# A new slot table for the state-space stage, three banks for its scans, and y in two banks by turns

## The chip, the cores and the metric

The program runs on one core of one Trainium2 chip. The metric is the device time of one execution in microseconds; lower is better.

## What is computed

Four layers follow one another on x (8 x 512 tokens of 256), each as x = x + layer(layernorm(x)): linear attention, a mixture of eight experts with one expert per token, a state-space layer, and the mixture of experts again. Only the state-space layer is touched. Cut to what matters:

```
xc, z = split(x @ in_proj_w.T)
u  = conv over 4 taps (512 -> 512 channels) of xc, + conv_b
dt = clip(sigmoid(u @ dt_w.T + dt_b), 1e-4, 1)
B, C = u @ B_w.T, u @ C_w.T                    # 16 states each
for every t:
    state = exp(dt * A) * state + dt * B * u + 1e-6     # 512 channels x 16 states
    y = sum over states(state * C) + D * u
out = (y * silu(z)) @ out_w.T
```

All of it is float32.

## The kernel before

Channels lie on partitions and time along the free axis, so the recurrence over 512 time steps of one quarter k (128 channels) and one state n is a single scan instruction on VectorE (DVE), `m_scan`, L1047. There are 8 batches x 16 states x 4 quarters = 512 scans. The program is written in **slots**: slot g = 64 b + 4 n + k holds scan g, and 64 slots are a batch b. The engines run their own instruction streams side by side and meet at semaphores.

What every slot holds:
- ScalarE (ACT): `m_decay`, exp(dt * A) for the scan three slots ahead (L612, ring of five buffers), and `m_input`, one of the four pieces of dt * B * u for the next group of four scans (L622).
- TensorE (PE): `m_spread`, four 128x128 transposes (L1091) that turn the input of scan g into a PSUM bank, 2 or 3 by turns, where the scan reads it. It waits for the scan two slots back.
- DVE: the scan. Its result goes into one of seven h buffers (the list H).
- GpSimd (POOL), once every four slots: `c_product` (L407) multiplies the four h quarters of state n by C; states 2 to 13 are then added onto state 0 or 1 by an accumulating DMA of 1 MB (`add_on`, L419), the last two by a sum on POOL (L417). A DMA waits for the last but one before it. SyncE (SP) loads the row of C for each state (L340), and in between stores the finished rows of the batch before.

Everything else of the layer is fitted between the scans, at slots that tables of numbers set; every engine walks through the same table in order:
- `CONV_AT`, `BC_AT`, `DT_AT`, `Z_AT`, `OUT_AT`: the slots at which PE issues the matmuls of conv (L1327), of B and C (L1341), of dt (L1359) for batch b + 1, of z (L1391) for b, and of the output of b - 1 (L1411, 256 wide, two of which count as one here). `UT_AT`, `DTT_AT`, `BT_AT`, `XT_AT`: turns by transposes of u (L1335), dt (L1376), B (L1369) and x.
- `UC_AT`, `UTC_AT`, `BCC_AT`, `TH_AT`, `ZTH_AT`, `NORM_AT`, `XTC_AT`: ACT's evacuations, the two passes of dt (L596, L598), the tanh of z (L604) and the norm.
- `SKIP_AT`, `ADD_AT`, `FINAL_AT`, `UPDATE_AT`, `CLIP_AT`, `WT_AT`, `BTC_AT`, `GATE_AT`: DVE's passes. y of a batch is made in PSUM in four banks, 4 to 7, one for each quarter: `m_skip` writes D * u (L988), `m_add` adds the even and the odd sum of POOL (L999), `m_final` multiplies by the gate (L1005). `m_clip` (L965) and `m_weigh` (L977) belong to dt, `m_gate` (L983) to z, `m_update` (L1014) adds the output matmul to x and then takes its statistics (L1020).

All matmuls other than the spreads share banks 0 and 1, so many wait for a bank that ACT or DVE has yet to read:

```
CONV_AT = ((0, 0, 1, 2, 2, 3, 4, 4), (5, 6, 6, 7, 8, 8, 9, 10), (10, 11, 12, 12, 13, 14, 14, 15),
           (16, 16, 18, 18, 20, 20, 22, 22))
DT_AT = ((32, 32, 34, 34), (40, 40, 41, 42), (46, 46, 47, 48), (52, 52, 53, 54))
DTT_AT = (38, 45, 51, 57)
TH_AT = (35, 43, 49, 55)
CLIP_AT = (36, 44, 50, 56)
```

Before the first scan the same table is walked for batch 0 alone (`m_prep(0, q)`), and behind the last one come the adds, finals and outputs of batch 7.

## Time and profile before

| | |
|---|---|
| median of 3 runs | 1716.4 us (1714.13 to 1721.19) |
| the profiled execution, its own time | 1717.43 us |
| its span, first to last instruction | 1715.3 us |
| mean granted TensorE clock | 0.925 |
| busy: PE, DVE, ACT, POOL | 85%, 65%, 56%, 53% of the span |
| DMA | 202.87 MB, mean 118 GB/s |

The profile is of one execution. Busy shares are over the whole program, in which the state-space layer is about one half; the profile's slices and the stretches that are asked of the trace tell the layers apart. In a row of the trace, what stands behind "idle before" is the time for which the engine stood still before the instruction, and the arrow names what ended it.

### The profile page before, as it was taken

Reading aid. Unit: us, or ns where it says so; the run is one execution under the profiler, and the core shown is the slowest. Engines: PE = TensorE matmul, PEld = TensorE weight load, DVE = VectorE, ACT = ScalarE, POOL = GpSimd, SP = SyncE. Lnnn points to the kernel's source line nnn. Section 1 sums busy time; section 2 is a strip of 40 time slices with the busy share of each in tenths; the row PEclk is TensorE's granted clock in tenths of the full one; section 3 lists DMA queues with packets and bytes.
Section 4 is the critical chain, followed back from the end, with each engine's and each line's share of the span. In section 5 each row is a group of like instructions: output and inputs, shape, how many; then the busy total and the mean of one; then the engine's idle time right before and its main releaser. Section 6 shows DMA issues by size and latency. Waiting matters only on the chain.

```text
span 1715.3 us, 21255 instructions
## 1 busy us (share of the span) xinstructions
PE 1453.1 (85%) x6310; PEld 930.3 (54%) x6311; DVE 1120.5 (65%) x1703; ACT 957.8 (56%) x1749; POOL 913.6 (53%) x417
## 2 busy tenths in 40 slices
PE   2899787999996978989889899898997773859997
PEld 1566584666642545545545555455554552836664
DVE  5566536444341677988878889888898985354443
ACT  1222120333323888888888888988888880203332
POOL 1111001344200578979879788797887995014442
PEclk9999958999998989999999999999999587579999
DMA  9300022111130386694966949759488495601120
GB/s 304 125 24 24 25 74 71 49 60 59 30 98 13 71 191 132 153 207 99 217 144 151 199 101 214 171 133 202 102 198 189 108 227 136 211 25 56 60 59 19
DMA packets 81315, 202.87 MB, mean 118 GB/s; under 512 B 9610, under 2 KB 40463, under 8 KB 68689
## 3 DMA queue, kind: packets, MB, share of 16 engines
q0 software_dynamic: 21376, 119.30, 32.3%
q1 hardware_dynamic: 55632, 78.91, 14.8%
q10 hardware_dynamic: 4224, 3.67, 0.7%
q8 instruction: 38, 0.62, 0.1%
q14 instruction: 45, 0.36, 0.1%
HBM read 84.14 MB, written 18.88 MB: 60 GB/s over the span
## 4 chain that ended last, share of the span: by engine, by line
PE 61%; DVE 15%; ACT 10%; issue 8%; DMA 2%; POOL 2%; SPq 1%; ACTq 1%; DVEq 0%; POOLq 0%
PE ps L1091 11%; PE ps L1261 8%; PE ps L1244 8%; PE ps L1327 7%; DVE arena L1047 6%; PE ps L1359 5%; ACT arena L612 4%; ACT arena L622 4%; PE ps L1116 3%; PE ps L1391 3%; PE ps L1296 3%; PE ps L1153 2%; PE ps L1107 2%; PE ps L1341 2%; PE ps L1189 2%
## 5 line engine op out<-in xcount | busy, mean ns | idle before, releaser
L1091 PEld LDWEIGHTS ps<-cst,arena 128*128 128x128 f32 x2836 | 361.2, 150 | 353.6 <-issue 216.0
L1091 PE MATMUL ps<-cst,arena 128*128 128x128 f32 x2836 | 461.0, 292 | 106.4 <-DVE arena L1047 31.3
L407 POOL TENSOR_TENSOR arena<-arena 128x2048 f32<-128x2048 f32 x98 | 450.1, 4594 | 162.0 <-DVE arena L1047 161.0
L1047 DVE TENSOR_TENSOR_SCAN arena<-arena,ps 128x512 f32<-128x512 f32 x392 | 467.6, 1211 | 99.4 <-PE ps L1091 95.5
L612 ACT ACTIVATE arena<-arena,a_neg 128x512 f32<-128x512 f32 x512 | 366.1, 715 | 83.0 <-DVE arena L1047 63.9
L622 ACT ACTIVATE arena<-arena,m_bt 128x512 f32<-128x512 f32 x512 | 362.9, 709 | 7.6 <-PE ps L1091 6.6
L1327 PE MATMUL ps<-arena,tapw 128*128 128x512 f32 x512 | 246.4, 598 | 0.0
L376 POOL DMA_INDIRECT arena<-rows,arena x78 | 75.7, 970 | 242.8 <-DVE arena L894 219.4
L529 ACT ACTIVATE arena<-ps,b1t 128x128 f32<-128x128 f32 x312 | 89.0, 368 | 168.0 <-PE ps L1091 104.6
L1047 DVE TENSOR_TENSOR_SCAN x<-arena,ps 128x512 f32<-128x512 f32 x120 | 143.9, 1212 | 38.2 <-PE ps L1091 36.7
L1261 PE MATMUL ps<-arena 128*128 x624 | 151.3, 385 | 6.5 <-ACT arena L529 3.1
L1244 PE MATMUL ps<-arena 128*128 x312 | 150.7, 606 | 1.0 <-issue 1.0
L407 POOL TENSOR_TENSOR x<-x,arena 128x2048 f32<-128x2048 f32 x30 | 137.8, 4593 | 24.7 <-DVE x L1047 24.0
L1359 PE MATMUL ps<-arena,dtw 128*128 128x512 f32 x256 | 135.3, 642 | 17.2 <-DVE arena L977 10.3
L1261 PEld LDWEIGHTS ps<-arena 128*128 128x128 f32 x624 | 112.3, 190 | 28.5 <-issue 16.4
L1327 PEld LDWEIGHTS ps<-arena,tapw 128*128 128x128 f32 x512 | 86.8, 192 | 55.0 <-issue 54.8
L919 DVE TENSOR_TENSOR arena<-ps,arena 128x256 f32<-128x256 f32 x78 | 33.1, 425 | 123.2 <-PE ps L1261 71.0
L900 DVE COPY arena<-ps 128x512 f32<-128x512 f32 x78 | 54.0, 692 | 76.6 <-PE ps L1244 71.7
L367 POOL TENSOR_TENSOR x<-x,arena 128x1024 f32 (+1 forms) x8 | 18.8, 2348 | 133.9 <-DVE arena L703 127.1
L390 POOL DMA_INDIRECT residual<-arena x39 | 39.5, 1014 | 91.2 <-DVE arena L926 91.2
L390 POOL DMA_INDIRECT out_x<-arena x39 | 39.5, 1013 | 90.3 <-DVE arena L926 90.3
L522 ACT ACTIVATE arena<-ps 128x256 f32<-128x256 f32 x78 | 30.0, 384 | 102.9 <-PE ps L1091 86.9
(152 smaller groups left out, 1691.8 us busy)
## 6 DMA issues: line engine op xcount, KB each, us to landing
...
arena<-c_rows SPq DMA_DIRECT2D x128, 256.0 KB, 3.6
...
```

The source lines that it names most:

```text
L376: g.indirect_dma_start(out=t_x[j % XB], out_offset=None, in_=xs[r], in_offset=bass.IndirectOffsetOnAxis(ap=idx[:, j:j + 1], axis=0))\
L390: g.indirect_dma_start(out=x_mid if r == 0 else T["out"].rearrange("b s d -> (b s) d"), out_offset=bass.IndirectOffsetOnAxis(ap=idx[:, j:j ...
L407: g.tensor_tensor(h, h, m_c[i % RC].unsqueeze(1).to_broadcast([P, KI, SEQ]), ALU.mult)\
L529: last = a.activation(t_ht[par][:, k, :], ps[4 + par][:, k * P:(k + 1) * P], ACT.Relu, bias=b1t[:, row(e), k:k + 1].rearrange("p a b -> p ...
L612: a.activation(m_a[g % RA], m_dt[b % 2][:, k, :], ACT.Exp, scale=a_neg[:, k, n:n + 1])\
L622: a.activation(m_dbt[i % 2][:, c, :], m_wt[b % 2][:, c, :], ACT.Copy, bias=1e-6, scale=m_bt[b % 2][:, c, n:n + 1]).then_inc(S("m_dbt"), 1)
L1047: v.tensor_tensor_scan(out=h[:, k, :], data0=m_a[g % RA], data1=ps[2 + g % 2][:, :], initial=0.0, op0=ALU.mult, op1=ALU.add).then_inc(S("m ...
L1091: return t.transpose(bank, src[:, k * P:(k + 1) * P], ident)
L1244: last = t.matmul(ps[2 + par][:, :], t_xt[par][:, k, :], w1[:, row(e), k, :].rearrange("p a h -> p (a h)"), start=(k == 0), stop=(k == KD ...
L1261: last = t.matmul(ps[6 + par][:, 0:D], t_ht[par][:, k, :], w2[:, row(e), k, :].rearrange("p a h -> p (a h)"), start=(k == 0), stop=(k == K ...
L1327: mm = t.matmul(ps[CONV_BANK[o]][:, :], tapw[:, k, d, o * P:(o + 1) * P], m_xt[n % 2][:, d, k:k + SEQ], start=(i == 0), stop=(i == TAPS * ...
L1359: mm = t.matmul(ps[DT_BANK[o]][:, :], dtw[:, k, o * P:(o + 1) * P], m_u[n % 2][:, k, :], start=(k == 0), stop=(k == KI - 1))
```

## The change

The work is the same; what changes is where it stands and in which bank:
- A new table. Conv, B and C, dt, output and z matmuls are spread over the slots at one matmul, or one and a half where halves of the output matmuls fit, a slot, with two in seven or so slots. The matmuls of B and C run between those of conv, each as soon as its quarter of u is there. The turn of dt stands two or three slots behind the clip, and the statistics of x in four slots of their own.
- Scans read their input from three banks (2, 3, 6) by turns, so a spread waits for the scan three slots back.
- y has banks 4 and 5 alone: quarters 0 and 1 are closed first (adds in slots 8, 9, 11, 12, finals in 13, 14), then quarters 2 and 3 in the same banks (skips in 14, 15, adds in 16 to 19, finals in 20, 21). Then the output matmuls use these two banks. In code: `m_close`.
- B, C and half of z have bank 7; dt uses banks 0 and 1 by turns. The waits follow the banks.
- SP stores the rows of the batch before behind the update that now stands in slot 49 (39 before), and its load of rows behind the last scans waits for the last final instead of the last add.

Lines of the changed kernel differ: spreads are L1108, conv L1344, B and C L1361, dt L1373 and its turn L1388, the scan L1056.

**PE, slots 0 to 4, while conv runs.** Before; the first row of each pair is the spread of one slot, ps2 and ps3 are the banks of the scans:

```order
L1091 MATMUL ps2<-cst,arena 128x128 x4
L1327 MATMUL ps0<-arena,tapw 128x512 x2
L1091 MATMUL ps3<-cst,arena 128x128 x4
L1327 MATMUL ps0<-arena,tapw 128x512
L1091 MATMUL ps2<-cst,arena 128x128 x4
L1327 MATMUL ps0<-arena,tapw 128x512 x2
L1091 MATMUL ps3<-cst,arena 128x128 x4
L1327 MATMUL ps0<-arena,tapw 128x512
L1091 MATMUL ps2<-cst,arena 128x128 x4
L1327 MATMUL ps0<-arena,tapw 128x512 x2
```

The same place after the change:

```order
L1108 MATMUL ps2<-cst,arena 128x128 x4
L1344 MATMUL ps0<-arena,tapw 128x512
L1108 MATMUL ps3<-cst,arena 128x128 x4
L1344 MATMUL ps0<-arena,tapw 128x512
L1108 MATMUL ps6<-cst,arena 128x128 x4
L1344 MATMUL ps0<-arena,tapw 128x512 x2
L1108 MATMUL ps2<-cst,arena 128x128 x4
L1344 MATMUL ps0<-arena,tapw 128x512
L1108 MATMUL ps3<-cst,arena 128x128 x4
L1344 MATMUL ps0<-arena,tapw 128x512
```

Two, one, two, one, two conv matmuls have become one, one, two, one, one, and bank 6 has come into the turn of the spreads.

**PE, before the first scan, where dt of batch 0 is made.** `dtw` is the weight of dt; the rows from `cst` with 128x128 turn its result (the row with 128x32 turns B). Before, from the first quarter of dt on:

```order
L1359 MATMUL ps0<-arena,dtw 128x512 x4
L1376 MATMUL ps0<-cst,arena 128x128 x4
L1359 MATMUL ps0<-arena,dtw 128x512 x2
L1369 MATMUL ps1<-cst,arena 128x32 x4
L1359 MATMUL ps0<-arena,dtw 128x512 x2
L1376 MATMUL ps0<-cst,arena 128x128 x4
L1359 MATMUL ps1<-arena,dtw 128x512 x4
L1376 MATMUL ps1<-cst,arena 128x128 x4
L1359 MATMUL ps0<-arena,dtw 128x512 x4
L1376 MATMUL ps0<-cst,arena 128x128 x4
```

After, from the second quarter on:

```order
L1373 MATMUL ps1<-arena,dtw 128x512 x3
L1381 MATMUL ps7<-cst,arena 128x32 x4
L1388 MATMUL ps0<-cst,arena 128x128 x4
L1373 MATMUL ps1<-arena,dtw 128x512
L1373 MATMUL ps0<-arena,dtw 128x512
L1388 MATMUL ps1<-cst,arena 128x128 x4
L1373 MATMUL ps0<-arena,dtw 128x512 x3
L1373 MATMUL ps1<-arena,dtw 128x512 x2
L1388 MATMUL ps0<-cst,arena 128x128 x4
L1373 MATMUL ps1<-arena,dtw 128x512 x2
L1388 MATMUL ps1<-cst,arena 128x128 x4
```

Before, all four matmuls of a quarter are followed at once by its turn; after, one to three matmuls of the next quarter, in the other bank, stand between, but for the last.

**DVE, from the first final pass of a batch on.** L1047 and L1056 are the scans, L1005 and L1016 the finals, L999 and L1010 the adds, L1000 a skip; ps4 to ps7 are the banks of y. Before, from slot 14 on:

```order
L1005 SCALAR_TENSOR_TENSOR arena<-ps4,arena 128x512
L1047 SCALAR_TENSOR_TENSOR x<-arena,ps3 128x512
L999 TENSOR_TENSOR ps7<-ps7,arena 128x512
L1005 SCALAR_TENSOR_TENSOR arena<-ps5,arena 128x512
L1047 SCALAR_TENSOR_TENSOR arena<-arena,ps2 128x512
L1005 SCALAR_TENSOR_TENSOR arena<-ps6,arena 128x512
L1047 SCALAR_TENSOR_TENSOR arena<-arena,ps3 128x512
L1005 SCALAR_TENSOR_TENSOR arena<-ps7,arena 128x512
```

After, from the final of quarter 0 (slot 13) on:

```order
L1016 SCALAR_TENSOR_TENSOR arena<-ps4,arena 128x512
L1056 SCALAR_TENSOR_TENSOR x<-arena,ps3 128x512
L1016 SCALAR_TENSOR_TENSOR arena<-ps5,arena 128x512
L1000 TENSOR_SCALAR ps4<-arena,mvec 128x512
L1056 SCALAR_TENSOR_TENSOR x<-arena,ps6 128x512
L1000 TENSOR_SCALAR ps5<-arena,mvec 128x512
L1056 SCALAR_TENSOR_TENSOR arena<-arena,ps2 128x512
L1010 TENSOR_TENSOR ps4<-ps4,x 128x512
L1056 SCALAR_TENSOR_TENSOR arena<-arena,ps3 128x512
L1010 TENSOR_TENSOR ps5<-ps5,x 128x512
```

Before, four finals end y in slots 14 to 17; after, two finals are followed by the skips of quarters 2 and 3 into the same banks, whose adds and finals reach to slot 21.

The diff, cut to its core:

```diff
-UT_AT = (7, 13, 19, 25)
-OUT_AT = ((24, 24, 24, 24, 26, 26, 26, 26), (36, 36, 36, 36, 38, 38, 38, 38))
-BC_AT = (28, 28, 30, 30)
+CONV_AT = ((0, 1, 2, 2, 3, 4, 5, 6), (7, 8, 8, 9, 10, 12, 13, 14), (14, 15, 16, 17, 18, 20, 21, 21),
+           (22, 23, 24, 26, 28, 29, 30, 31))
+UT_AT = (9, 17, 24, 34)
+OUT_AT = ((23, 25, 25, 27, 29, 31, 32, 32), (38, 41, 41, 42, 42, 45, 47, 47))
+BC_AT = (11, 19, 27, 36)
+DT_AT = ((33, 34, 35, 36), (37, 38, 39, 40), (43, 44, 45, 46), (48, 49, 50, 51))
+DTT_AT = (40, 44, 50, 55)
-Z_AT = ((42, 43), (48, 49), (54, 55), (58, 58))
+Z_AT = ((52, 53), (54, 55), (56, 57), (58, 59))
...
+TH_AT = (37, 41, 47, 52)
+ZTH_AT = (54, 56, 58, 60)
...
-ADD_AT = ((8, 9, 10, 11), (12, 13, 14, 15))
-FINAL_AT = (14, 15, 16, 17)
-UPDATE_AT = (27, 39)
-SKIP_AT = (34, 36, 38, 40)
+ADD_AT = ((8, 9, 16, 17), (11, 12, 18, 19))
+FINAL_AT = (13, 14, 20, 21)
+UPDATE_AT = (33, 49)
+STAT_AT = (34, 35, 52, 54)
+SKIP_AT = (44, 50, 14, 15)
+CLIP_AT = (38, 42, 48, 53)
+WT_AT = (41, 45, 51, 56)
...
-BC_BANK, BT_BANK, DT_BANK, DTT_BANK, Z_BANK = 1, 1, (0, 0, 1, 0), (0, 0, 1, 0), (1, 0, 1, 1)
+XT_BANK, CONV_BANK, UT_BANK, OUT_BANK = (0, 1), (0, 1, 0, 1), (0, 1, 0, 1), (4, 5)
+BC_BANK, BT_BANK, DT_BANK, DTT_BANK, Z_BANK = 7, 7, (0, 1, 0, 1), (0, 1, 0, 1), (7, 0, 7, 1)
+SCAN_BANK = (2, 3, 6)
...
+        def added(b, odd, k):
+            return 2 * KI * b + 4 * (k // 2) + 2 * odd + k % 2 + 1
...
-            sp.wait_ge(S("m_add"), 2 * KI * BATCH)
+            sp.wait_ge(S("m_y"), KI * BATCH)
...
             def m_uevac(n, o):
+                if n >= 2 and o >= 2:
+                    a.wait_ge(S("m_y0"), KI * (n - 2) + o + 1)
...
             def m_skip(b, k):
+                if k >= 2:
+                    v.wait_ge(S("m_y"), KI * b + k - 1)
+                elif b:
+                    v.wait_ge(S("m_xupd"), 2 * (b - 1) + k + 1)
-                v.tensor_scalar(ps[4 + k][:, :], m_u[b % 2][:, k, :], mvec[:, 2, k:k + 1], None, ALU.mult)\
+                v.tensor_scalar(ps[4 + k % 2][:, :], m_u[b % 2][:, k, :], mvec[:, 2, k:k + 1], None, ALU.mult)\
...
+            def m_close(b, q):
+                for odd in range(2):
+                    if q in ADD_AT[odd]:
+                        m_add(b, odd, ADD_AT[odd].index(q))
+                if q in FINAL_AT:
+                    m_final(b, FINAL_AT.index(q))
+                if q in SKIP_AT[2:4]:
+                    m_skip(b, SKIP_AT.index(q))
...
-            for odd in range(2):
-                for k in range(KI):
-                    m_add(BATCH - 1, odd, k)
-            for k in range(KI):
-                m_final(BATCH - 1, k)
+            for q in range(FINAL_AT[-1] + 1):
+                m_close(BATCH - 1, q)
...
             def m_bcmm(n, k):
-                if k == 0:
-                    t.wait_ge(S("m_utc"), KI * (n + 1))
+                t.wait_ge(S("m_u"), KI * n + k + 1)
...
             def m_out(b, h, i):
                 if i == 0:
                     t.wait_ge(S("m_y"), KI * (b + 1))
-                    if h == 0 and b < BATCH - 2:
-                        t.wait_ge(S("m_utc"), KI * (b + 2) + 3)
...
             def m_spread(g):
-                if g >= 2:
-                    t.wait_ge(S("m_scan"), g - 1)
+                if g >= 3:
+                    t.wait_ge(S("m_scan"), g - 2)
                 for c in range(CPB):
-                    last = turned(ps[2 + g % 2][:, c * P:(c + 1) * P], m_dbt[g // KI % 2][:, c, :], k, c)
+                    last = turned(ps[SCAN_BANK[g % 3]][:, c * P:(c + 1) * P], m_dbt[g // KI % 2][:, c, :], k, c)
```

## Rows read from the trace of the kernel before

**Rows 1.** The scans: duration min/median/max in ns, first and last start

```profile
L1047 DVE TENSOR_TENSOR_SCAN arena<-arena,ps x392: 1190/1212/1222, 558.8 to 1424.1; 128x512 f32<-128x512 f32 x196
```

**Rows 2.** Busy time by stretch; PE, PEld, DVE, ACT, POOL, clock, DMA share, GB/s

```profile
558.70:672.30 113.60, 98.85 (x422) 55.50 (x421) 85.06 (x81) 95.09 (x155) 79.13 (x28) 0.92 0.66 144
672.30:780.60 108.30, 97.20 (x454) 58.50 (x453) 93.90 (x100) 96.03 (x156) 92.25 (x31) 1.00 0.73 161
780.60:890.50 109.90, 98.82 (x454) 58.97 (x453) 93.85 (x99) 95.96 (x156) 92.08 (x31) 0.98 0.72 163
...
1326.90:1425.40 98.50, 70.88 (x301) 48.52 (x300) 88.51 (x91) 78.22 (x124) 92.69 (x31) 0.71 0.76 173
```

**Rows 3.** Timeline of PE, slots 2 and 3 (start, duration; one matmul is two records)

```profile
783.90 1.88 PE L1327 MATMUL ps<-arena,tapw 128*128 128x512 f32 x4
785.62 0.60 PE L1091 MATMUL ps<-cst,arena 128*128 128x128 f32 x4
786.06 1.02 PE L1327 MATMUL ps<-arena,tapw 128*128 128x512 f32 x2
```

**Rows 4.** Timeline of DVE, slots 3 and 11

```profile
786.26 2.52 DVE L1047 TENSOR_TENSOR_SCAN arena<-arena,ps 128x512 f32<-128x512 f32 x2 [0.94 <-PE ps L1091]
...
800.51 1.22 DVE L1047 TENSOR_TENSOR_SCAN arena<-arena,ps 128x512 f32<-128x512 f32 x1
801.65 0.67 DVE L999 TENSOR_TENSOR ps<-ps,x 128x512 f32<-128x512 f32 x1
802.23 1.21 DVE L1047 TENSOR_TENSOR_SCAN x<-arena,ps 128x512 f32<-128x512 f32 x1
```

**Rows 5.** Timeline of ACT, dt, decay, input and tanh of z

```profile
876.52 0.66 ACT L596 ACTIVATE ps<-ps,mvec 128x512 f32<-128x512 f32 x1 [0.43 <-PE ps L1359]
...
877.71 0.71 ACT L612 ACTIVATE arena<-arena,a_neg 128x512 f32<-128x512 f32 x1
...
878.94 0.58 ACT L604 ACTIVATE arena<-ps 128x512 f32<-128x512 f32 x1
879.41 0.71 ACT L612 ACTIVATE arena<-arena,a_neg 128x512 f32<-128x512 f32 x1
```

**Rows 6.** Timeline of POOL, from the last two products of a batch on

```profile
775.63 4.52 POOL L407 TENSOR_TENSOR x<-x,arena 128x2048 f32<-128x2048 f32 x1 [1.60 <-DVE x L1047]
...
793.85 9.05 POOL L407 TENSOR_TENSOR arena<-arena 128x2048 f32<-128x2048 f32 x2
...
820.98 0.88 POOL L419 DMA_DIRECT2D arena<-arena  x1 [0.30 <-POOL arena L407]
...
826.72 0.88 POOL L419 DMA_DIRECT2D arena<-arena  x1 [0.30 <-POOL arena L407]
```

**Rows 7.** Timeline of PE, slots 40 to 51: waits for a bank and for dt

```profile
846.23 1.98 PE L1359 MATMUL ps<-arena,dtw 128*128 128x512 f32 x4 [1.43 <-DVE arena L977]
...
856.88 0.66 PE L1376 MATMUL ps<-cst,arena 128*128 128x128 f32 x4 [1.22 <-DVE arena L965]
...
867.65 0.66 PE L1376 MATMUL ps<-cst,arena 128*128 128x128 f32 x4 [1.23 <-DVE arena L965]
```

**Rows 8.** DMA issues: the rows of C (KB each, median us to landing)

```profile
arena<-c_rows SPq DMA_DIRECT2D x128, 256.0 KB, 3.6
```

**Rows 9.** The accumulating DMAs of L419

```profile
DMA to landing us min/median/max: 7.0/8.3/10.5
```

**Rows 10.** Timeline of PE before the first scan

```profile
517.61 3.62 PE L1341 MATMUL ps<-arena,bcw 128*32 128x512 f32 x8 [0.69 <-ACT arena L589]
...
526.95 0.66 PE L1376 MATMUL ps<-cst,arena 128*128 128x128 f32 x4 [2.09 <-DVE arena L965]
528.39 3.62 PE L1359 MATMUL ps<-arena,dtw 128*128 128x512 f32 x4 [0.78 <-DVE arena L977]
```

**Rows 11.** Timeline of DVE behind the last scan

```profile
1438.27 2.49 DVE L999 TENSOR_TENSOR ps<-ps,arena 128x512 f32<-128x512 f32 x4 [6.54 <-POOL arena L417]
1440.67 2.47 DVE L1005 SCALAR_TENSOR_TENSOR arena<-ps,arena 128x512 f32<-128x512 f32 x4
```

More of the change, by code:

```diff
@@ L1015, in m_update, with m_stat @@
                     .then_inc(S("m_xupd"), 1)
-                if h == 0:
-                    return
-                v.wait_ge(S("m_xupd"), 2 * b + 2)
-                for c in range(CPB):
-                    last = v.bn_stats(out=stats[:, place(b) + c, :], in_=x[:, kept(b) + c, :])
-                last.then_inc(S("m_stat"), 1)
+            def m_stat(b, c):
+                v.wait_ge(S("m_xupd"), 2 * b + c // 2 + 1)
+                v.bn_stats(out=stats[:, place(b) + c, :], in_=x[:, kept(b) + c, :]).then_inc(S("m_stat"), 1)
             def m_pre(n, q):
@@ L1053, in m_all @@
                         m_scan(SLOTS * b + q, clip)
-                        for odd in range(2):
-                            if b and q in ADD_AT[odd]:
-                                m_add(b - 1, odd, ADD_AT[odd].index(q))
-                        if q in SKIP_AT:
+                        if b:
+                            m_close(b - 1, q)
+                        if q in SKIP_AT[0:2]:
                             m_skip(b, SKIP_AT.index(q))
@@ L1060, in m_all @@
                             m_pre(b + 1, q)
-                        if b and q in FINAL_AT:
-                            m_final(b - 1, FINAL_AT.index(q))
                         if b and q in UPDATE_AT:
                             m_update(b - 1, UPDATE_AT.index(q), OUT_BANK[UPDATE_AT.index(q)])
+                        if b and q in STAT_AT:
+                            m_stat(b - 1, STAT_AT.index(q))
                         if q in GATE_AT:
@@ L1076, in _ @@
                 m_all(False)
-            for odd in range(2):
-                for k in range(KI):
-                    m_add(BATCH - 1, odd, k)
-            for k in range(KI):
-                m_final(BATCH - 1, k)
-            m_update(BATCH - 1, 0, 0)
-            m_update(BATCH - 1, 1, 1)
-            feed(1, "m_stat", BATCH)
+            for q in range(FINAL_AT[-1] + 1):
+                m_close(BATCH - 1, q)
+            for h in range(2):
+                m_update(BATCH - 1, h, OUT_BANK[h])
+            for c in range(CPB):
+                m_stat(BATCH - 1, c)
+            feed(1, "m_stat", NCH)
         @block.tensor
@@ L1338, in m_bcmm @@
             def m_bcmm(n, k):
-                if k == 0:
-                    t.wait_ge(S("m_utc"), KI * (n + 1))
+                if k == 0 and n == 1:
+                    t.wait_ge(S("m_btc"), 1)
+                if k == 0 and n >= 2:
+                    t.wait_ge(S("m_sz"), KI * (n - 2) + 3)
+                t.wait_ge(S("m_u"), KI * n + k + 1)
                 mm = t.matmul(ps[BC_BANK][0:2 * NS, :], bcw[:, k, :], m_u[n % 2][:, k, :], start=(k == 0), stop=(k == KI - 1))
@@ L1382, in m_zmm @@
                 if k == 0:
-                    if o == 0:
-                        t.wait_ge(S("m_xupd" if end else "m_btc"), 2 * b if end else b + 2)
-                    if o == 1:
-                        t.wait_ge(S("m_xupd" if end else "m_wt"), 2 * b - 1 if end else KI * (b + 1) + 2)
+                    if o == 0 and b:
+                        t.wait_ge(S("m_sz"), KI * b)
+                    if o == 0 and not end:
+                        t.wait_ge(S("m_btc"), b + 2)
+                    if o == 1 and not end:
+                        t.wait_ge(S("m_wt"), KI * (b + 1) + 3)
                     if o == 2:
-                        t.wait_ge(S("m_sz" if end else "m_wt"), KI * b + 1 if end else KI * (b + 1) + 3)
-                    if o == 3:
-                        t.wait_ge(S("m_sz"), KI * b + 3)
+                        t.wait_ge(S("m_sz"), KI * b + 1)
+                    if o == 3 and not end:
+                        t.wait_ge(S("m_wt"), KI * (b + 1) + 4)
                 mm = t.matmul(ps[Z_BANK[o]][:, :], zw[:, k, o * P:(o + 1) * P], m_xt[b % 2][:, k, PAD:],
@@ L1461, in _ @@
             t.wait_ge(S("m_far"), 1)
-            t.matmul(ps[7][:, 0:1], ones, far_sum[:, :], start=True, stop=True).then_inc(S("m_farsum"), 1)
+            t.matmul(ps[5][:, 0:1], ones, far_sum[:, :], start=True, stop=True).then_inc(S("m_farsum"), 1)
             for k in range(KD):
```

76 lines of the change are left out of this document (25 added, 51 removed).

## The prediction

> **What bounds the kernel now.** I read the busy time of the engines by stretch first. The state-space layer, slot 0 of batch 0 to slot 63 of batch 7, starts at 558.8 us and its last scan starts at 1424.1 [rows 1]: half of the span, and all that the change touches. An undisturbed batch takes 108.3 us, with PE busy 97.2, ACT 96.0, DVE 93.9 and POOL 92.3 [rows 2]. No engine fills the batch and four are near it, so the question is not which engine is slow but how their work falls into slots. Some batches take 109.9 at a clock of 0.98; batch 0 takes 113.6 at 0.92, batch 7 98.5.
>
> Then the pace of each engine, from one start to the next. PE: two 512-wide matmuls 1.72, so 0.86 each; the four transposes that spread an input 0.44 [rows 3]; an output matmul of half the width I take as 0.43. DVE: a scan 1.14, another pass over a bank 0.58 [rows 4]. ACT: decay and input together 1.23 a slot, the gate's tanh 0.47, the two passes of dt 1.19 [rows 5]. POOL: two products with two closing sums 18.2, two products without a sum 9.1, a product with its accumulating DMA 5.74 (820.98 to 826.72) [rows 6].
>
> Times the counts of the code these make a batch of 91.3 on PE (64 spreads, 60 matmuls, 16 halves, 10 turns and the small one), about 92.5 on DVE, 92.7 on ACT, and on POOL 9.1 + 12 x 5.74 + 18.2 = 96.2. The change leaves all four as they are. Their largest is the floor of a batch.
>
> What is lost is seen in two places. In slots 0 to 15 PE has two matmuls in every second slot: 0.44 + 1.72 = 2.16, then 1.30. DVE needs 1.14 in these slots and has only two banks to be ahead with; it idles 0.94 in front of every pair of scans [rows 4]. In slots 40 to 57 PE stops for 1.2 to 1.4 us again and again, at the turn of dt and where a bank comes free [rows 7]: tanh, clip and turn stand in successive slots.
>
> **The table, part by part.** As a bound I add for each engine what four successive slots hold, take the largest of the three, and sum the 16 groups: 106.4 before, 103.7 after; in groups of eight 103.4 and 100.5. Measured before: 108.3, or 1.9 and 4.9 above. So the table alone is worth about 2.8, and the third bank lets groups be longer, so the truth after should stand nearer to the groups of eight.
>
> By stretches of the new table, each with the engine that has most to do:
> - Slots 8 to 21, DVE: 14 scans and 14 other passes, 14 x 1.14 + 14 x 0.58 = 24.1. PE has 21.6.
> - Slots 22 to 36, PE: the output matmuls of slot 23 wait for the last final pass in slot 21, so PE starts there without a lead: 13 matmuls, 8 halves, 13 spreads, 2 turns = 21.2, and 0.5 to the next scan: 21.7.
> - Slots 37 to 51: PE 12 matmuls, 8 halves, 15 spreads, 3 turns and the small one = 22.0; ACT 15 x 1.23 + 3 x 1.19 + 0.47 = 22.5; DVE 15 x 1.14 + 9 x 0.58 + the copy = 22.5. I take 22.5.
> - Slots 52 to 63, ACT: 12 x 1.23 + 1.19 + 10 x 0.48 = 20.7. DVE has 17.8, PE 13.5.
> - Slots 0 to 7, ACT: 8 x 1.23 + 0.58 = 10.4. PE has 11.2, but comes from a light stretch with up to three spreads done.
>
> Sum 99.4. Friction in place of 4.9: I take half, 2.6, since the waits of [rows 7] go (the turn now stands two or three slots behind the clip) and three engines are level in slots 37 to 51. That gives **102.0 a batch**. Batches 1 to 6 take 654.6 now (1326.9 less 672.3, rows 2) and 612 then: -42.6. Batch 0 has no closing passes and no output matmuls: 52.2 on PE for slots 0 to 36 plus 43.2 on ACT = 95.4, and 4.6 for friction and its slow clock, 100 against 113.6: -13.6.
>
> **Batch 7 and POOL.** POOL starts batch 7 behind the closing sums of batch 6 and then never rests: 98.5 against its 96.2. Scans that come sooner don't move its end. I put 0 here; in the other batches 102 leaves it 5.8 us.
>
> **The waits that are new.** (a) y has two banks, so the skip of quarters 2 and 3 waits for the finals of 0 and 1, and the odd sum is added from slot 11 on (12 before). POOL gives it 18.2 after the last but one group of scans (775.6 to 793.9, rows 6), about 12 us after slot 63; slot 11 falls at 10.4 + three slots with two passes and one with one = 16. Spare 3 to 4, cost 0; behind it on DVE stand all scans, so each us beyond costs a us. (b) SP stores the last batch and loads the row of C for n = 12 only behind the update of slot 49 (39 before). The load takes 3.6 us to land [rows 8], the store stands before it, and product 12 may start some 2.5 to 3 us behind that update: POOL loses 1 to 2 of its 5.8. Cost 0; with no spare it would be 7 to 14 us in all. (c) The h buffers are reused 17 slots behind their last scan, 27 us; product and DMA take 4.5 + 0.3 + 8.3 to 10.5 [rows 9]. Cost 0. (d) bn_stats in four places in place of one: same work.
>
> **Before the first scan.** PE waits 2.1 us behind each of four dt blocks, and 0.7 to 0.9 at four more places [rows 10]: 11.5. In the new order block 1 of dt covers the tanh of block 0 but for nothing, one matmul covers 0.86 of the next, two cover 1.7 of the third, the last is bare: 0 + 1.25 + 0.4 + 2.1 + 0.8, and 0.8 for u before dt: 5.4. -6.1. Bounds: 0 (if ACT, in order, is what counts) and -8.
>
> **Behind the last scan.** The last sum of POOL is followed by 8 passes of 0.6 on DVE [rows 11], then by the output matmuls. Now two quarters are closed and only then the other two: 2 even adds are done sooner, 12 passes remain: 7.3 for 4.9, +2.4. The 2 MB load of rows starts that much later; the norm that needs it starts later too.
>
> **Sum.** -42.6 - 13.6 - 6.1 + 2.4 = -59.9. The profiled execution took 1717.4, its span 1715.3; the median of the runs is 1716.4, 1.0 below it and within their spread of 7. 1717.4 - 59.9 = 1657.5; I forecast **1657 us**. Friction of 0.6 or of 4.6 makes it 12 less or more, and batch 0 adds 2: 1638 to 1672 is this case.
>
> **The rivals.**
> - *Most friction stays* (0.22): ACT feeds the spreads of the next group with no slot to spare, and level engines wait for each other in turn. Then the four-slot bound holds, 103.7 + 1.9 = 105.6 a batch, 3.6 x 6 + 3.6 more: 1682. For it: before, only this bound came near. Against: a third bank, and [rows 7] gone.
> - *Down to POOL's floor* (0.06): 96.2 a batch, 5.8 x 6 + 3.8 less: 1618. It asks that three engines of 92 interlock almost without loss.
> - *The change does not do what it says* (0.04): wait (a) decides. If POOL is late by 11 us rather than 3, DVE waits 8 a batch and the period is 110 as before: 1657 + 7 x 7.7 = 1711. Against: POOL idled 1.6 us before its last product but one, so it is not behind [rows 6].
> - *Slower, by DMA* (0.03): POOL issues an accumulation only when the last but one has landed. Issues two products apart are 11.5 us, landings at most 10.5 [rows 9]. If denser traffic (a share of 0.73 of 108.3 us, so 0.78 of 102) stretches landings, POOL's batch is 38 + 5.1 landings: no gain from 14 us on, and at 15 us 114.5 a batch, 801 for seven in place of 768: 1747.
> - *Slower, by PE's clock* (0.03): if the even table, with a short gap in every slot, let PE fall to 1.2 GHz in slots 8 to 21, its 21.6 would be 43 in place of DVE's 24.1: +19 x 7, 1790. It decides from 10 us of PE's work a batch at the low level. Against: with PE busy nine tenths the granted clock was 0.98 to 1.00, and 0.71 only in batch 7, with PE busy 70.9 of 98.5 us [rows 2]; after the change 91.3 of 102 is work.
>
> The Trainium skill, "TensorE: Matmul & The Clock Gate", section "A second HAM failure mode: psum-queue depth-cycling", speaks against the change: a kernel that went through PSUM banks in turn left PE idle for moments between groups, and its clock went back and forth. By that rule the last rival would be the forecast and the time 1790. The trace of before already goes through two banks in turn with short gaps at 1.00, so I do not follow it.
>
> **Chances and range.** Forecast 0.62, and the five rivals as given. Under 0.5% (8.6 us) a measurement of this kernel can't tell a change from none. The first three cases are faster: 0.90; the fourth is no change: 0.04; the last two slower: 0.06. From 1638 to 1690 lie the forecast and most of the first rival, 0.8.
>
> **What would show it.** 512 scans with batches near 102 us, PE busy nine tenths in them; almost no idle time of DVE for spreads in slots 0 to 7; no 1.2 us waits at the turn of dt; POOL with 4 to 6 us idle a batch; first scan near 553; 7 us of passes between POOL's last sum and the output matmuls. Wrong if DVE waits for POOL in slot 11, if POOL waits for landings, if batches stay at 105 or more with PE waiting for ACT's inputs every fourth slot, or if the granted clock falls inside batches 1 to 6.

## The result, and the profile after

The changed kernel takes **1656.7 us**, the median of 5 runs (1655.4 to 1664.5), against 1716.4 before: a ratio of 0.966, with a 95% interval from 0.962 to 0.969. That is the 1657 of the forecast. The profiled execution took 1664.5, its span is 1662.5, and so it is the slowest of the five (more on that at the end of the explanation). Against the span of before (1715.3) it is 52.8 shorter.

The busy time by stretch of the changed kernel, read as in [rows 2]: batches 0 to 3, and batch 7, which ends with its last scan:

```profile
549.00:647.50 98.50, 90.07 (x422) 52.65 (x421) 84.05 (x79) 93.50 (x155) 81.22 (x28) 0.98 0.76 168
647.50:749.10 101.60, 94.74 (x454) 57.79 (x453) 93.58 (x99) 95.39 (x157) 89.37 (x30) 1.00 0.75 165
749.10:852.00 102.90, 96.04 (x454) 58.48 (x454) 93.59 (x99) 95.30 (x157) 92.27 (x31) 0.98 0.77 175
852.00:954.90 102.90, 97.60 (x454) 59.64 (x453) 93.59 (x99) 95.51 (x156) 93.48 (x32) 0.96 0.77 176
...
1262.00:1354.40 92.40, 60.92 (x301) 44.62 (x299) 87.10 (x91) 78.12 (x124) 85.03 (x29) 0.78 0.75 170
```

DVE and ACT do the work of before, to within a per cent, in the batches that compare best (DVE 93.6 for 93.9, ACT 95.4 for 96.0), in 101.6 to 102.9 us in place of 108.3 to 109.9. The time came out of the gaps. The starts of all 512 scans tell which (us, batch 1 before and after):

| slots | before | after | what the prediction took as bound |
|---|---|---|---|
| 0 to 7 | 14.2 | 11.2 | ACT 10.4, with PE at 11.2 |
| 8 to 21 | 24.2 | 24.7 | DVE 24.1 |
| 22 to 36 | 22.5 | 22.7 | PE 21.7 |
| 37 to 51 | 27.7 | 23.7 | ACT and DVE 22.5 |
| 52 to 63 | 19.7 | 19.3 | ACT 20.7 |

Two stretches give all of it, and they are those where the prediction saw the loss. In slots 0 to 7 both times are just PE's work: 12 matmuls of 0.86 and nine times four transposes at 0.44 (eight spreads and a turn of u) make 14.3 before, 9 matmuls and eight spreads 11.3 after. There DVE had idled 0.94 before every pair of scans [rows 4]. Timeline of DVE of the changed kernel, slots 0 to 8 of batch 1:

```profile
647.61 3.82 DVE L1056 TENSOR_TENSOR_SCAN x<-arena,ps 128x512 f32<-128x512 f32 x3 [0.54 <-PE ps L1108]
652.37 1.22 DVE L1056 TENSOR_TENSOR_SCAN x<-arena,ps 128x512 f32<-128x512 f32 x1 [0.94 <-PE ps L1108]
653.66 6.41 DVE L1056 TENSOR_TENSOR_SCAN arena<-arena,ps 128x512 f32<-128x512 f32 x5
```

The wait of 0.94 is left only behind slot 2, the one with two matmuls. In slots 37 to 51 PE had stopped for a bank and for the turn of dt [rows 7]: 5.8 us of waits in these slots of batch 2, of which 2.4 are for the clip and the rest for banks and inputs; in the changed kernel none of 0.1 us or more is left. Timeline of PE now, the first turn of dt (slot 40), and the first row from slot 37 on that has a wait, in slot 56 or so:

```profile
710.36 0.66 PE L1108 MATMUL ps<-cst,arena 128*128 128x128 f32 x4
710.85 0.60 PE L1388 MATMUL ps<-cst,arena 128*128 128x128 f32 x4
711.28 1.02 PE L1373 MATMUL ps<-arena,dtw 128*128 128x512 f32 x2
...
735.37 0.66 PE L1108 MATMUL ps<-cst,arena 128*128 128x128 f32 x4 [1.52 <-ACT arena L630]
```

Turn and next matmul follow without a gap, for 25 us on end.

**What did not go as predicted** is in three other places. First, PE's clock falls at the ends of batches. Slots 0 to 7 of batch 2, by stretch:

```profile
749.10:761.50 12.40, 12.40 (x52) 7.09 (x52) 9.65 (x8) 10.87 (x19) 12.24 (x4) 0.90 0.33 84
```

The granted clock is 0.90 and the stretch takes 12.4 in place of 11.2. What PE did before it fell, at the end of batch 2 and the start of batch 3:

```profile
848.72 1.09 PE L1108 MATMUL ps<-cst,arena 128*128 128x128 f32 x8 [1.69 <-DVE arena L991]
850.92 1.11 PE L1108 MATMUL ps<-cst,arena 128*128 128x128 f32 x4 [1.11 <-ACT arena L630]
851.83 1.92 PE L1344 MATMUL ps<-arena,tapw 128*128 128x512 f32 x2
853.53 0.81 PE L1108 MATMUL ps<-cst,arena 128*128 128x128 f32 x4
854.18 1.02 PE L1344 MATMUL ps<-arena,tapw 128*128 128x512 f32 x2
```

PE has nothing but spreads left there and waits 1.7 and 1.1. The next four transposes and one matmul take 1.11 and 1.92 where 0.66 and 1.02 are usual: the step of 0.86 has become 1.70, the level of 1.2 GHz. The granted clock is 0.50 from about 850.7 to 854.0, some 3.3 us, then 1.00 again.

Second, POOL now waits for a row of C. The rows of C by tile, before and then after:

```profile
  POOL arena L407: 0.4, 2
  POOL x L407: 0.2, 1
DMA to landing us min/median/max: 1.6/3.6/5.5
```

```profile
  POOL arena L413: 26.8, 7
  POOL x L413: 4.2, 1
DMA to landing us min/median/max: 1.6/3.8/11.0
```

Seven waits of 3.8 to 4.9 us, one in each of batches 1 to 7, and one of 0.2: 31 us in all. In batch 7, timeline of SP's queue and of POOL (the second row of the queue is two loads, the first of them issued at 1336.21):

```profile
1335.80 0.37 SPq L308 DMA_DIRECT2D rows<-x  x1
1336.21 5.66 SPq L346 DMA_DIRECT2D arena<-c_rows  x2
```

```profile
1346.56 4.55 POOL L413 TENSOR_TENSOR arena<-arena 128x2048 f32<-128x2048 f32 x1 [3.79 <-DMA arena<-c_rows]
```

The load is issued 0.4 us behind the store, and the product that needs it starts 10.3 us later. Third, the end. DVE behind POOL's last sum, and the output matmuls, which are to be read against [rows 11]:

```profile
1376.22 1.30 DVE L1010 TENSOR_TENSOR ps<-ps,arena 128x512 f32<-128x512 f32 x2 [7.73 <-POOL arena L423]
1377.42 1.28 DVE L1016 SCALAR_TENSOR_TENSOR arena<-ps,arena 128x512 f32<-128x512 f32 x2
1378.62 1.40 DVE L1000 TENSOR_SCALAR ps<-arena,mvec 128x512 f32<-128x512 f32 x2
1379.93 1.29 DVE L1010 TENSOR_TENSOR ps<-ps,x 128x512 f32<-128x512 f32 x2
1381.12 1.28 DVE L1010 TENSOR_TENSOR ps<-ps,arena 128x512 f32<-128x512 f32 x2
1382.32 1.28 DVE L1016 SCALAR_TENSOR_TENSOR arena<-ps,arena 128x512 f32<-128x512 f32 x2
```

```profile
1383.65 10.21 PE L1415 MATMUL ps<-outw,arena 128*128 128x256 f32 x32 [32.60 <-DVE arena L1016]
```

Twelve passes, as predicted, in 7.4 us; and the output matmuls take 10.21 us in place of 8.78 before, at a granted clock of 0.70 in place of 0.81.

### The profile page after: what moved, and what is told of

It reads as the page before. It is cut to its first block, busy times and chain, and to the rows that moved or that the text cites. A ratio compares the mean times of both kernels' runs of the same rounds, so it can differ in the third digit from the quotient of the medians.

```text
span 1662.5 us, 21266 instructions
## 1 busy us (share of the span) xinstructions
PE 1431.1 (86%) x6310; PEld 929.5 (56%) x6311; DVE 1117.9 (67%) x1703; ACT 951.9 (57%) x1749; POOL 915.3 (55%) x417
## 4 chain that ended last, share of the span: by engine, by line
PE 63%; DVE 12%; ACT 10%; issue 8%; POOL 4%; DMA 2%; SPq 1%; ACTq 1%; POOLq 0%; DVEq 0%
PE ps L1108 13%; PE ps L1344 10%; PE ps L1278 9%; PE ps L1261 8%; DVE arena L1056 4%; PE ps L1373 4%; ACT arena L620 4%; ACT arena L630 3%; PE ps L1133 3%; PE ps L1313 3%; POOL arena L413 2%; PE ps L1415 2%; PE ps L1170 2%; PE ps L1124 2%; PE ps L1206 2%
## 5 line engine op out<-in xcount | busy, mean ns | idle before, releaser
L1108 PEld LDWEIGHTS ps<-cst,arena 128*128 128x128 f32 x2836 | 373.7, 151 | 407.6 <-issue 255.2
L1108 PE MATMUL ps<-cst,arena 128*128 128x128 f32 x2836 | 458.5, 291 | 113.4 <-ACT arena L630 48.4
L413 POOL TENSOR_TENSOR arena<-arena 128x2048 f32<-128x2048 f32 x98 | 460.3, 4699 | 119.0 <-DVE arena L1056 91.5
L1056 DVE TENSOR_TENSOR_SCAN arena<-arena,ps 128x512 f32<-128x512 f32 x392 | 471.2, 1212 | 62.1 <-PE ps L1108 54.6
L1344 PE MATMUL ps<-arena,tapw 128*128 128x512 f32 x512 | 260.4, 608 | 0.0
L1056 DVE TENSOR_TENSOR_SCAN x<-arena,ps 128x512 f32<-128x512 f32 x120 | 143.9, 1211 | 18.6 <-PE ps L1108 16.5
L1373 PE MATMUL ps<-arena,dtw 128*128 128x512 f32 x256 | 130.7, 598 | 2.2 <-ACT arena L585 1.2
L1415 PE MATMUL ps<-outw,arena 128*128 128x256 f32 x256 | 74.3, 407 | 37.6 <-DVE arena L1016 37.6
L1344 PEld LDWEIGHTS ps<-arena,tapw 128*128 128x128 f32 x512 | 85.0, 195 | 29.5 <-issue 28.4
L528 ACT ACTIVATE arena<-ps 128x256 f32<-128x256 f32 x78 | 29.9, 384 | 104.5 <-PE ps L1108 87.1
## 6 DMA issues: line engine op xcount, KB each, us to landing
arena<-in_W SPq DMA_DIRECT2D x32, 512.0 KB, 10.2
```

Of the source, the lines that this page charges most:

```text
L413: g.tensor_tensor(h, h, m_c[i % RC].unsqueeze(1).to_broadcast([P, KI, SEQ]), ALU.mult)\
L1056: v.tensor_tensor_scan(out=h[:, k, :], data0=m_a[g % RA], data1=ps[SCAN_BANK[g % 3]][:, :], initial=0.0, op0=ALU.mult, op1=ALU.add).then_i ...
L1108: return t.transpose(bank, src[:, k * P:(k + 1) * P], ident)
L1344: mm = t.matmul(ps[CONV_BANK[o]][:, :], tapw[:, k, d, o * P:(o + 1) * P], m_xt[n % 2][:, d, k:k + SEQ], start=(i == 0), stop=(i == TAPS * ...
L1373: mm = t.matmul(ps[DT_BANK[o]][:, :], dtw[:, k, o * P:(o + 1) * P], m_u[n % 2][:, k, :], start=(k == 0), stop=(k == KI - 1))
L1415: mm = t.matmul(ps[OUT_BANK[h]][:, (c % 2) * D:(c % 2) * D + D], m_sz[:, k, c * P:(c + 1) * P], outw[:, k, :], start=(k == 0), stop=(k == ...
```

## The experiments

The theory at the start: half of the gain per batch is the even table, most of the rest the third bank of the scans, which lets DVE run ahead; the turn of dt two slots behind the clip gives the third share. (All four turns stand exactly two slots behind the clip, at 40, 44, 50 and 55 against 38, 42, 48 and 53, not "two or three" as the description of the change has it; before it was two for the first and one for the others.) The first versions undo these one by one. Batch times below are from start to start of slot 0.

**Two banks.**

```diff
-SCAN_BANK = (2, 3, 6)
+SCAN_BANK = (2, 3)
-                if g >= 3:
-                    t.wait_ge(S("m_scan"), g - 2)
+                if g >= 2:
+                    t.wait_ge(S("m_scan"), g - 1)
```

> The changed kernel with its scans on two banks (2 and 3) in place of three; table and y as changed. Theory of the prediction (the third bank lets PE be further ahead, so the longer groups decide): batches go from 102.5 us to 105 or 106, time 1673 to 1683. Rival (with an even table two banks are enough, the table alone is the gain): batches within 1 us, time 1655 to 1664.

Measured: 1656.5 us, ratio 0.963 [0.959, 0.967]; batches 98.6, 101.6, 102.9, 102.2, 101.1, 101.2, 99.9, and every eight slots take what they take with three banks, wherever the granted clock is the same. In batches 4 to 6 of this trace it was 1.00, and slots 0 to 7 took 11.2 us in place of 11.6 to 11.9. The third bank is worth nothing in this table.

**The old bunching.** Conv in pairs in every second slot, as before:

```diff
-CONV_AT = ((0, 1, 2, 2, 3, 4, 5, 6), (7, 8, 8, 9, 10, 12, 13, 14), (14, 15, 16, 17, 18, 20, 21, 21),
-           (22, 23, 24, 26, 28, 29, 30, 31))
+CONV_AT = ((0, 0, 2, 2, 4, 4, 6, 6), (8, 8, 10, 10, 12, 12, 14, 14), (16, 16, 18, 18, 20, 20, 21, 21),
+           (22, 22, 24, 24, 28, 28, 30, 30))
```

> The changed kernel with the conv matmuls put back into pairs (two in every second slot); three banks kept. Theory (evenness and the third bank replace each other: either lets a scan find its input): batches longer by 0 to 1.5 us, time 1657 to 1668. Rival (evenness is the gain, whatever the banks): longer by 3 us or more, time 1678 and above.

Measured: 1663.8 us, 0.968 [0.965, 0.972]; batches 99.6, 101.6, 102.9, 102.8, 102.6, 102.6, 101.7, from batch 1 on those of the changed kernel. The intervals of the two kernels overlap. The edit isn't quite clean: slots 0 to 7 hold 8 matmuls and not 9, and take 11.4 where PE's work is 10.4, so the bunches cost 1 us there and the matmul moved out gives 0.9 back, in slots where it is covered. In sum a batch doesn't change.

**Both.** The two edits together.

> Both: conv in pairs and two banks for the scans. Theory (they replace each other): much more than the sum of the two alone, batches of 106 us or more, time 1683 to 1695. Rival (each has its own price): the sum of what e1 and e2 lose.

Measured: 1662.9 us, 0.969 [0.966, 0.972]; batches without a fall of the clock take 102.0. Slots 16 to 23 take 13.3 in place of 12.5 and slots 24 to 31 12.6 in place of 12.3. So a third bank and an even table do stand in for each other, but both together are worth about 1 us a batch: in slots 8 to 21 DVE's own passes cover most of what PE does unevenly. What made slots 0 to 7 short is above all their number of matmuls: 9 now, or 8 in these two versions, where the old table had 12. No version put the 12 back, so this rests on the sum of PE's work above, which meets both measured times to 0.1 us.

**The turn one slot earlier.**

```diff
-DTT_AT = (40, 44, 50, 55)
+DTT_AT = (39, 43, 49, 54)
```

> The changed kernel with the four turns of dt one slot earlier, next to the clip as before the change. Theory of the prediction (the waits of 1.2 us at the turn were part of the friction): they come back, batches longer by 1.5 to 4 us, and the way to the first scan by about 3: time 1670 to 1688. Rival (three banks hide them from DVE): batches the same to 0.5 us, time 1657 to 1663.

Measured: 1670.9 us, 0.974 [0.971, 0.978]; batches 103.2, 104.5, 103.0, 103.4, 104.3, 101.8 from batch 1 on, 1.9 more without the clock's part. Timeline of PE of this kernel, the waits of one batch:

```profile
712.63 0.66 PE L1388 MATMUL ps<-cst,arena 128*128 128x128 f32 x4 [0.17 <-DVE arena L973]
720.00 0.66 PE L1388 MATMUL ps<-cst,arena 128*128 128x128 f32 x4 [1.00 <-DVE arena L973]
729.54 0.66 PE L1388 MATMUL ps<-cst,arena 128*128 128x128 f32 x4 [0.66 <-DVE arena L973]
```

0.17 + 1.00 + 0.66 = 1.8: PE's waits for the clip go over one to one into the batch, since PE, ACT and DVE are level in slots 37 to 51. Of all parts that were undone this one is worth most: 1.9 of the 4.0 us that slots 37 to 51 gained. The other half, which the waits for banks of [rows 7] would explain, was not undone.

**The same distance in the old kernel.** If the distance is what counts, the old table should gain by it:

```diff
-DTT_AT = (38, 45, 51, 57)
+DTT_AT = (38, 46, 52, 58)
-WT_AT = (39, 46, 52, 58)
+WT_AT = (39, 47, 53, 59)
```

> The kernel before with only the last three turns of dt and the weighing behind them one slot later. Theory (the turn next to the clip cost the new table 1.9 us a batch, so it costs the old one as much): batches of 106.2 to 106.8 in place of 108.3, 12 to 15 us in all, 1701 to 1705. Rival (in the old table PE's pairs of matmuls set the pace of these slots anyway): batches of 108, 1714 to 1718.

Measured: 1753.9 us, 1.022 [1.021, 1.024]: **38 us slower**, a plain miss. Batches take 113.0 to 118.3, slots 40 to 63 of batches 1 to 6 45.5 to 48.2 in place of 40.7 to 42.5. Timelines of PE and then of DVE, slots 58 and 59:

```profile
892.08 3.43 PE L1391 MATMUL ps<-arena,zw 128*128 128x512 f32 x4 [1.63 <-DVE arena L983]
```

```profile
896.41 1.22 DVE L1047 TENSOR_TENSOR_SCAN arena<-arena,ps 128x512 f32<-128x512 f32 x1 [3.26 <-PE ps L1091]
```

The three waits for the clip are indeed gone, but others have grown: from slot 38 on PE waits 13.2 us in batch 2 in place of 10.2. In the old kernel z and dt share banks 0 and 1, and the last quarter of z now meets the moved turn in slot 58: PE waits for the gate that frees z's bank, then issues z's two matmuls (four records), and the turn and the spread stand behind them. The two take 3.43 us, about twice the usual time, at a granted clock of 0.57, so part of the loss is the clock. That the distance can be had in the new table because B, C and half of z have bank 7 and dt alternates is argued from this and not shown: a version of the changed kernel with z on banks 0 and 1 again was not run, and the new table also puts z behind dt's last matmuls.

**Where POOL's wait comes from.** Store two states later:

```diff
-                    if n == NS - 4 and b:
+                    if n == NS - 2 and b:
```

> The changed kernel with SP's store of the last batch's rows (and its wait for the update of slot 49) moved from ahead of the row of C for state 12 to ahead of that for state 14. Theory (that wait holds back the load, POOL stops for 4 us at product 12, and only batch 7 feels it, where POOL has nothing to spare): the wait of product 12 goes in all batches, batches 1 to 6 stay at 102 to 103, and POOL's last sum comes 3 to 4 us sooner: 1653 to 1654. Rival (POOL's lag at the end of a batch holds up the adds of slot 8 to 11 of the next): batches shorter too, 1650 or less. Other rival (nothing waits for POOL there): no difference.

Measured: 1657.9 us, 0.967 [0.966, 0.969]. The waits are half as long in sum (16.6 us in place of 31.0; none in batches 1 and 3), and in batch 7 the wait moved two products on; timeline of POOL:

```profile
1358.54 4.49 POOL L413 TENSOR_TENSOR arena<-arena 128x2048 f32<-128x2048 f32 x1 [4.07 <-DMA arena<-c_rows]
```

The trace of the changed kernel has two causes for its waits. In batches 1 to 6 it is the update of slot 49, as the prediction had it. Timelines of batch 2: the update on DVE, the store on SP's queue, the product on POOL:

```profile
828.69 0.67 DVE L1025 TENSOR_TENSOR x<-ps,x 128x512 f32<-128x512 f32 x1
```

```profile
829.43 0.37 SPq L308 DMA_DIRECT2D rows<-x  x1
```

```profile
836.17 4.54 POOL L413 TENSOR_TENSOR arena<-arena 128x2048 f32<-128x2048 f32 x1 [4.34 <-DMA arena<-c_rows]
```

POOL had made room for the row at 824.9, but the store goes out only 0.1 us behind the update, and the load behind the store: 5 us late. It then lands in 6.2 us (6.1 to 6.7 in these six batches). In batch 7 the update had ended 2.4 us before the store, and the store went out right behind POOL's product, so nothing held it; there it is the landing of 10.2 us. Landings of 7.7 to 11.3 are also what is left in most batches with the store two states later, where the update is long done.

Why that load takes 10.2 us is open. The DMA engines have no room around it; but they had none in batch 7 before either, where the load behind the store landed in 4.8 us. The stretch before, then after:

```profile
1392.00:1413.00 21.00, 16.31 (x71) 10.01 (x72) 18.86 (x18) 19.76 (x33) 18.23 (x7) 0.84 1.02 226
```

```profile
1330.00:1351.00 21.00, 16.49 (x80) 10.20 (x79) 19.75 (x22) 17.60 (x29) 16.21 (x6) 0.92 1.02 235
```

And four versions (both undone, the turn one slot earlier, and the two kinds with constant matmuls) have loads of 7.6 to 9.7 us with no store in front of them for 11 us or more, and in the first of these the load right behind the store of batch 7 landed in 5.2.

**The store at the end of the batch's loads.** It then stands in front of no load that POOL is close to:

```diff
-                    if n == NS - 4 and b:
-                        sp.wait_ge(S("m_xupd"), 2 * b)
-                        store_rows(1, b - 1)
...
+                if b:
+                    sp.wait_ge(S("m_xupd"), 2 * b)
+                    store_rows(1, b - 1)
```

> The changed kernel with SP's store of the last batch's rows at the end of the batch, behind the row of C for state 15, where POOL issues no accumulations for 18 us. Theory now (the row of C behind the store takes 10 us to land because the DMA engines are full of accumulations, not because SP waits for the update of slot 49): POOL waits for no row of C in batch 7, and its last sum comes 3.5 to 4 us sooner counted from slot 0 of batch 7 (110 us instead of 114); batches 1 to 6 unchanged; time 1653. Rival (the waits for rows of C only move to another product, as when the store was moved by two states): still 114.

Measured: 1654.6 us (1654.4 to 1655.8), 0.965 [0.963, 0.966]. POOL's waits for rows of C are 0.7 in all (31.0 in the changed kernel): no load waits for the update any more, and none takes longer than 5.3 us to land in this trace. From slot 0 of batch 7 to POOL's last sum it takes 108.9, with the store in place 114.1, before 111.3. The trace gains 5.2: the wait of 3.8 in batch 7, and 1.4 by which POOL, held up in batch 6, came late to the sums that open batch 7. In the medians it is 2, with intervals that overlap.

**Four banks for the last y.** In batch 7 alone quarters 2 and 3 go to banks 0 and 1, which are free then:

```diff
+            def y_bank(b, k):
+                return (4, 5, 0, 1)[k] if b == BATCH - 1 else 4 + k % 2
```

> The changed kernel, but batch 7 has four banks for y (0 and 1 are free by then): skips and even adds are done before POOL's last sum. Theory: the passes behind that sum go from 7.3 us back to 4.9, time 2.4 less, 1654. Rival (the output matmuls or the 2 MB load of rows decide the end): 0 to 0.5 less.

Measured: 1659.8 us, 0.967 [0.966, 0.968]. From POOL's last sum to the norm it takes 21.1 in place of 24.1, but the whole doesn't show it; both at once (the next) don't either.

> e5 and e6 together: if they act at different places, the sum of both, 1650 to 1652. If one covers the other, no more than the larger.

Measured: 1660.5 us, 0.966 [0.965, 0.968].

**Is it the clock?** Four matmuls of a constant in slots 60 to 63, into bank 7, read by nobody:

```diff
+                    if q in (60, 61, 62, 63) and b < BATCH - 1:
+                        if q == 60:
+                            t.wait_ge(S("m_sz"), KI * b + 3)
+                        t.matmul(ps[7][:, :], ident, cst[:, 0:512], start=True, stop=True)
```

> The changed kernel with one more 512-wide matmul of constants into bank 7 in each of slots 60 to 63 of batches 0 to 6 (its result is not read). Theory (the fall of the granted clock at the end of most batches, 0.96 to 0.98, comes from the light slots of PE before it and makes the first conv matmuls slow, slots 0 to 7 taking 11.7 to 12.5 us instead of 11.2): clock 1.00 in batches 2 to 5, each 1 us shorter, 1651 to 1653 in all. Rival (the 3.4 us of matmuls a batch delay the spreads more than that): time 1660 or more.

Measured: 1659.9 us, 0.969 [0.967, 0.970]; batches 103.2, 103.1, then 102.2. Slots 0 to 7 take 11.2 in every batch from 1 on, at a clock of 1.00, but slots 56 to 63 of batches 0 to 5 take 13.6 to 14.6 in place of 12.7 to 13.6: from slot 0 of batch 0 to slot 0 of batch 7 it is 712.9 us, against 713.0 in the changed kernel, so the cure costs what it brings.

**All three, with smaller matmuls** (256 wide, in slots 61 to 63), the store at the end and the four banks:

```diff
+                    if q in (61, 62, 63) and b < BATCH - 1:
+                        if q == 61:
+                            t.wait_ge(S("m_sz"), KI * b + 3)
+                        t.matmul(ps[7][:, 0:256], ident, cst[:, 0:256], start=True, stop=True)
```

> The changed kernel with the store at the end of the batch, four banks for y in batch 7, and one 256-wide matmul of constants in slots 61, 62 and 63 of batches 0 to 6 (1.3 us a batch in place of 3.4). Theory: POOL's end 3.5 us sooner, the passes behind it 2.4 shorter, and the clock at 1.00 across the ends of the batches with slots 56 to 63 longer by 0.3 at most: batches of 101.2 to 101.6, 4 to 6 us less there; together 1645 to 1648. If the matmuls are too few to keep the clock: batches as they were, 1650 to 1652.

Measured: **1643.7 us** (1642.2 to 1649.1), 0.959 [0.957, 0.961]; it beats both kernels. Batches 101.2, 101.2, 102.0, 100.9, 101.2, 101.4. The same stretch as above, slots 0 to 7 of batch 2, by stretch, and PE at the end of batch 2:

```profile
749.90:761.20 11.30, 11.30 (x52) 6.57 (x51) 9.78 (x9) 11.15 (x19) 11.22 (x3) 1.00 0.22 61
```

```profile
848.21 0.66 PE L1120 MATMUL ps<-cst,arena 128*128 128x128 f32 x4 [1.26 <-DVE arena L993]
848.71 0.60 PE L1493 MATMUL ps<-cst 128*128 128x256 f32 x2
...
850.91 1.02 PE L1356 MATMUL ps<-arena,tapw 128*128 128x512 f32 x2
```

**The same without the constant matmuls.**

> The edit: the version e11 (rows of C stored at the end, four banks for the last batch's outputs) without its three extra constant matmuls in each of batches 0 to 6. Theory: the extra matmuls kept the clock up across the ends of batches. Then the batches are those of the changed kernel again, up to 102.8 each where the clock falls (e11: 100.9 to 102.0), and the time is 1648 to 1653. Rival: they did nothing that the time shows, and e11 owes its gain over e9 (1654.6) to the four banks at the end, which were worth 3 us in the profile of e6: the time is 1643 to 1647.

Measured: 1649.4 us (1645.2 to 1651.6), 0.960 [0.957, 0.962]. In the traces the theory holds: the batches are again 101.6, 102.8, 102.9, 102.8, 102.6, 101.7, slots 0 to 7 take 12.4 at a clock of 0.91, and from slot 0 of batch 0 to slot 0 of batch 7 it is 712.9 us, with the matmuls 706.4. Batch 7 gives 2.3 of these 6.5 back (111.2 to POOL's last sum in place of 108.9, with a wait for a row of C of 2.4 in it). In the times the two can't be told apart: their intervals overlap.

## Why the prediction was right, and where it was not

The total is right to a microsecond, and part of that is luck. In the profiled executions the terms sum to -52.9 where -59.9 was forecast; the medians differ by 59.7, because the profiled execution of the changed kernel is 7.8 above its median and that of before 1.0. And terms that were off have opposite signs. In the profiled executions:

| step | predicted | measured |
|---|---|---|
| batches 1 to 6 | -42.6 | -40.1 |
| batch 0 | -13.6 | -15.1 |
| conv of batch 0 to the first scan | -6.1 | -7.9 |
| batch 7 to POOL's last sum | 0 | +2.8 |
| from there to the norm of the second mixture of experts | +2.4 | +3.8 |
| before conv, and from that norm to the end | 0 | -1.8, +5.4 |

- **The batch.** 102.0 was forecast and 102.4 measured, but as two numbers that were both off. Where the clock holds at 1.00 (batches 4 and 5 with two banks) a batch takes 101.1 to 101.2; no batch of the changed kernel has it from end to end. So friction over the bound by groups of eight (100.5) is 0.6 to 0.7 and not 2.6. And the falls of the clock at the ends of batches add 0.5 to 1.8, which the sum had nothing for; the last sentence of the prediction named a falling clock as what would make it wrong. Level engines lose less on each other than I took.
- **The stretches.** Slots 8 to 21 and 22 to 36 came out 0.6 and 1.0 above their bounds, 37 to 51 1.2 above, 52 to 63 1.4 below, though ACT never idles there, so some of the work that the sum put into these slots is done outside them. In slots 0 to 7 the forecast let PE profit from a lead; it has none, and takes its own 11.2.
- **"The third bank lets groups be longer"** failed as a reason. With two banks the batches are the same. The groups of eight were the better bound all the same, since DVE's passes cover most of PE's unevenness. The rival that most friction stays (1682) fell with it.
- **The turn of dt** was right: the waits of [rows 7] are gone, and undoing it costs 1.9 a batch. What I had not seen is that it can't be had alone: moved by itself in the old kernel, it costs 38 us.
- **Wait (a)**, the odd sum in slot 11, cost nothing, as forecast.
- **Wait (b)** had the right place, and in batches 1 to 6 the right cause, but its size was taken too small: a landing of 3.6 us [rows 8] where 6.1 to 6.7 was measured, and so a loss of 1 to 2 for POOL where it was 4.2 to 4.9. POOL's slack takes most of it, but from batch 6 1.4 us go on into batch 7. In batch 7 the cause is another, a landing of 10.2. Together that is the 5.2 that moving the store takes off.
- **Batch 7** was put at 0 because POOL "never rests" in it. It did rest before, 1.9 us in all, once for a scan:

```profile
1396.85 4.52 POOL L407 TENSOR_TENSOR arena<-arena 128x2048 f32<-128x2048 f32 x1 [1.66 <-DVE arena L1047]
```

  With the store moved it rests 0.2, and its first closing sum starts 0.9 us before slot 0 in place of 0.3. Within rounding these 1.7 and 0.6 are the gain of 2.4 (111.3 to 108.9). So the "0" was a gain of 2.4 and a loss of 5.2.
- **Before the first scan** the waits for dt were forecast as 0 + 1.25 + 0.4 + 2.1 + 0.8, and 0.8 for u:

```profile
517.86 1.12 PE L1373 MATMUL ps<-arena,dtw 128*128 128x512 f32 x2 [0.78 <-ACT arena L585]
...
529.65 0.66 PE L1388 MATMUL ps<-cst,arena 128*128 128x128 f32 x4 [1.04 <-DVE arena L973]
...
534.97 0.66 PE L1388 MATMUL ps<-cst,arena 128*128 128x128 f32 x4 [0.37 <-DVE arena L973]
...
539.44 0.70 PE L1388 MATMUL ps<-cst,arena 128*128 128x128 f32 x4 [2.09 <-DVE arena L973]
541.02 1.94 PE L1108 MATMUL ps<-cst,arena 128*128 128x128 f32 x8 [0.88 <-DVE arena L985]
```

  5.2 in all, against 5.4: a count of what stands between a matmul and its turn gave the waits. The stretch itself is 7.9 shorter where -6.1 was forecast; the other 1.6 were not followed.
- **Behind the last scan** the passes are as forecast; the 1.4 more are the output matmuls at a lower clock.
- **The clock rival** (1790) did not come. By the Trainium skill, "TensorE: Matmul & The Clock Gate", section "A second HAM failure mode: psum-queue depth-cycling", banks taken in turn would have let the clock go back and forth; here three banks, and two in the first experiment, gave batches at 0.96 to 1.00, though the banks turn in every slot; the falls come at the ends of batches, where PE has only spreads left and waits 1 to 2 us.

**The 5.4 at the end.** From the norm to the end the profiled executions of all fourteen kernels take 256.7 to 258.4 us (before, and eight others) or 261.8 to 262.1 (the changed kernel, and four others), though no edit touches that part. The router's matmuls, at the start of it, tell them apart; the changed kernel and then the one with the later store:

```profile
1405.30 3.42 PE L1313 MATMUL ps<-wr,arena 128*128 128x8 f32 x16
```

```profile
1404.06 1.85 PE L1313 MATMUL ps<-wr,arena 128*128 128x8 f32 x16
```

and from 1480 to 1500 the granted clock is 0.78 in the one and 1.00 in the other. The granted clock of the output matmuls, just before the norm, puts all fourteen in order: at 0.80 to 0.83 the rest takes 256.7 to 256.9 us (five kernels), at 0.75 to 0.76 258.3 to 258.4 (four), at 0.70 to 0.74 261.8 to 262.1 (five). So the stretch goes with the clock that it finds; no version changed that clock alone. That would be some 5 of the 8 by which the profiled execution of the changed kernel is above its median (the other executions have no profile), and it is more than the 3 that four banks at the end bring. What sets the clock of the output matmuls stays open.
